# Causal attention of a fused two-layer kernel: head-wise 5 KB writes of the relative scores, a third staging pair, and value products ahead of the turns

## What is computed

```
Q = LN(x) Wq + bq ; K = ctx Wk + bk ; V = ctx Wv + bv        (per head, 512 x 16)
QEr = Q Er^T                      (512 x 512, Er is 512 x 16)
Srel = skew(QEr)                  (row s shifted so that column t holds Q[s] . Er[511 - s + t])
attn = softmax(causal((Q K^T + Srel) / 4)) ; out = attn V ; x = x + out
```

## Time and profile before

| what | us |
|---|---|
| median of 3 runs | 1227.47 |
| lowest, highest | 1227.22, 1229.96 |
| profiled execution, own time | 1220.86 |
| its span in the trace | 1219.0 |
| mean granted TensorE clock | 0.933 |
| causal stage, first `relative` to last scores | 57 to 358 |

### The profile page before, as it was taken

How to read it: one execution, slowest core, us unless ns; L and a number is a source line. 1 busy time by engine, 2 the same in 40 slices (tenths; PEclk the granted TensorE clock), 3 DMA queues, 4 the chain that set the end, 5 groups by cost and what they waited for, 6 DMA issues and landing times. The chain is left out here.

```text
span 1219.0 us, 22097 instructions
## 1 busy us (share of the span) xinstructions
PE 1068.6 (88%) x6978; PEld 665.8 (55%) x6979; DVE 661.2 (54%) x1993; ACT 635.3 (52%) x1245; POOL 199.1 (16%) x466
## 2 busy tenths in 40 slices
PE   7999999999997868999999991547999999987487
PEld 5556555555554567999999991312333333325254
DVE  4428778777776521121111102857666666774697
ACT  2457677776742422222223330516777777762797
POOL 0000000000000022122223210002222223230232
PEclk9959999999898979999999996869999999998798
DMA  5098899888966637566666654253111111100001
GB/s 181 10 302 280 281 311 293 302 272 287 295 226 225 226 118 278 190 216 216 216 216 221 230 192 147 92 184 109 49 46 48 46 45 45 47 26 9 0 32 39
DMA packets 92239, 199.56 MB, mean 164 GB/s; under 512 B 8392, under 2 KB 49608, under 8 KB 86152
## 3 DMA queue, kind: packets, MB, share of 16 engines
q1 hardware_dynamic: 88424, 188.46, 47.3%
q0 software_dynamic: 3744, 10.23, 2.2%
HBM read 134.82 MB, written 63.83 MB: 163 GB/s over the span
## 5 line engine op out<-in xcount | busy, mean ns | idle before, releaser
L775 DVE CUSTOM_DVE_ANT_0 unused<-mpsS,mask_bias 128x512 bf16<-128x512 f32 x256 | 172.1, 691 | 82.3 <-PE mpsS L708 81.9
L1516 ACT ACTIVATE hT<-ph,w 128x128 f32<-128x128 f32 x312 | 89.0, 368 | 205.1 <-PE ph L1490 186.5
L802 ACT ACTIVATE mPT<-mpsB 128x512 f32<-128x512 f32 x256 | 152.5, 597 | 80.8 <-PE mpsB L715 74.6
L1490 PE MATMUL ph<-xT,w 128*128 128x128 f32 x1248 | 151.1, 281 | 6.2 <-DMA w<-in_w1p 6.0
L1490 PEld LDWEIGHTS ph<-xT,w 128*128 128x128 f32 x1248 | 146.8, 197 | 8.6 <-issue 8.4
L1535 DVE TENSOR_TENSOR xn<-py,b 128x256 f32<-128x256 f32 x39 | 16.6, 425 | 244.9 <-PE py L1500 244.9
L1500 PE MATMUL py<-w,hT 128*128 x624 | 141.2, 379 | 0.7 <-DVE xn L1535 0.7
L650 ACT ACTIVATE scores<-scores,nm 128x512 f32<-128x512 f32 (+3 forms) x256 | 125.4, 554 | 10.5 <-DVE nm L621 10.5
L1500 PEld LDWEIGHTS py<-w,hT 128*128 128x128 f32 x624 | 115.6, 190 | 15.2 <-issue 1.1
L643 ACT COPY stage<-psE 128x1024 f32<-128x1024 f32 (+1 forms) x90 | 78.7, 874 | 83.6 <-PE psE L533 67.6
L708 PE MATMUL mpsS<-mqk 96*128 96x512 bf16 x256 | 100.5, 394 | 20.4 <-DMA mqk<-packed 17.3
(11 more groups left out here) (261 smaller groups left out, 1614.5 us busy)
## 6 DMA issues: line engine op xcount, KB each, us to landing
w<-in_w1p SPq DMA_DIRECT2D x39, 1028.0 KB, 5.6
rel<-stage SPq DMA_DIRECT2D x64, 512.0 KB, 7.5
bias<-rel SPq DMA_DIRECT2D x44, 640.0 KB, 6.0
x<-rel SPq DMA_DIRECT2D x20, 640.0 KB, 5.9
mqk<-packed SPq DMA_DIRECT2D x64, 192.0 KB
rel<-stage SPq DMA_DIRECT2D x32, 256.0 KB, 7.1
w<-in_w2p SPq DMA_DIRECT2D x8, 1024.0 KB, 12.5
b<-in_b SPq DMA_DIRECT2D x39, 128.0 KB, 5.7
```

The lines of the kernel that those rows point to most:

```text
L775: nc.vector.tensor_tensor_reduce(out=unused[:, i, :], in0=psS[i % 2][:, :], in1=mask_bias[:, i, :], scale=1.0, scalar=-3.0e38, op0=ALU.add ...
L802: nc.scalar.activation(PT[r][:, j, :], psB[j % 2][:, :], ACT.Exp, scale=1.0 / 4).then_inc(s_exp, 1)
L1490: mm = nc.tensor.matmul(ph[half][:, q * P:(q + 1) * P], w1[i][:, dk * F + f * P:dk * F + (f + 1) * P], xT[i][:, dk, :], start=(dk == 0), s ...
L1516: g = nc.scalar.activation(hT[i][:, f, :], ph[half][:, q * P:(q + 1) * P], ACT.Gelu, bias=w1[i][:, DK * F + f:DK * F + f + 1])
```

## The change

1. DRAM tensors are per head (eight of 128 x 1280) and each head is written by one DMA of 128 rows of 5 KB; a pair is 2 write DMAs in place of 3. The row pitch of the skewed read is 1279 elements in place of 2559.
2. A read of a head waits for that head's write alone.
3. SyncE's step order becomes: both reads of pair n+4, then both writes of pair n+5. The writes wait for all three units' copies.
4. Staging has three pairs of buffers. The third pair's two heads lie apart (one in x, one in the memory of mask_bias, which the early weights wkv and the heads buffer now share), so for every third pair ScalarE copies each unit with two instructions in place of one. ScalarE waits once a pair, at unit 0, for the two writes of three pairs before.
5. On TensorE, in each unit, `weigh` and (in unit 2) `vals.turn` come ahead of `turn_probs`.
6. SyncE waits for the last writes before it loads wkv.

```diff
-    rel = [dram(f"rel_{r}", (P, 2, REL_W), F32) for r in range(RING)]
+    rel = [dram(f"rel_{r}", (P, REL_W), F32) for r in range(ROUND)]
...
+            STAGES = 3
...
-                vals = Values(ctx, "a")
+                vals = Values(ctx, "a", wkv_flat[:, REL_W:REL_W + S])
...
-                s_wr = [[sem(f"s_wr{r}_{u}") for u in range(NU)] for r in range(RING)]
+                s_wr = [sem(f"s_wr{r}") for r in range(ROUND)]
...
+                def stage_of_head(p, h):
+                    if p % STAGES < 2:
+                        return stage[p % STAGES][:, h, :]
+                    return (spare[:, 2 * REL_W:3 * REL_W], wkv_flat[:, 0:REL_W])[h]
...
                     def read(p):
-                        for u in range(NU):
-                            sp.wait_ge(s_wr[p % RING][u], 16 * (p // RING + 1))
-                        sp.sem_inc(s_seen_sp, 1)
                         for h in range(2):
+                            slot = (2 * p + h) % ROUND
+                            sp.wait_ge(s_wr[slot], 16 * (2 * p // ROUND + 1))
+                            sp.sem_inc(s_seen_sp, 1)
                             if p >= len(bias):
                                 sp.wait_ge(s_soft, piece(p - len(bias), NU - 1, h) + 1)
-                            skewed = bass.AP(rel[p % RING].ap().tensor, P - 1 + h * REL_W, [[2 * REL_W - 1, P], [1, REL_W]])
-                            sp.dma_start(bias[p % len(bias)][:, h, :], skewed).then_inc(s_rd[(2 * p + h) % ROUND], 16)
-
-                    def write(p, u):
-                        cols = slice(512 * u, 512 * u + WU[u])
-                        sp.wait_ge(s_eev, NU * p + u + 1)
-                        if p >= RING:
-                            for h in range(2):
-                                m = 2 * (p - RING) + h
-                                sp.wait_ge(s_rd[m % ROUND], 16 * (m // ROUND + 1))
-                        sp.dma_start(rel[p % RING][:, :, cols], stage[p % 2][:, :, cols]).then_inc(s_wr[p % RING][u], 16)
+                            skewed = bass.AP(rel[slot].ap().tensor, P - 1, [[REL_W - 1, P], [1, REL_W]])
+                            sp.dma_start(bias[p % len(bias)][:, h, :], skewed).then_inc(s_rd[slot], 16)
+
+                    def write(p):
+                        sp.wait_ge(s_eev, NU * (p + 1))
+                        for h in range(2):
+                            slot = (2 * p + h) % ROUND
+                            wait(sp, s_rd[slot], 16 * (2 * p // ROUND))
+                            sp.dma_start(rel[slot][:, :], stage_of_head(p, h)).then_inc(s_wr[slot], 16)
 
                     for n in range(-REL, NP - SOFT):
-                        early, back = pair_at(n, REL), pair_at(n, READ)
-                        if early is not None:
-                            write(early, 0)
-                        if back is not None:
-                            read(back)
-                        if early is not None:
-                            write(early, 1)
-                            write(early, 2)
+                        if (p := pair_at(n, READ)) is not None:
+                            read(p)
+                        if (p := pair_at(n, REL)) is not None:
+                            write(p)
+                    for m in range(NBH - ROUND, NBH):
+                        sp.wait_ge(s_wr[m % ROUND], 16 * (m // ROUND + 1))
...
-                            if late is not None:
-                                turn_probs(late, u)
                             if 0 <= g < NBH // GROUP and u < 2:
...
-                        if n % 2 == 0 and 0 <= n // 2 - 2 < NBH // GROUP:
-                            vals.turn(pe, n // 2 - 2, 0)
+                            if u == 2 and n % 2 == 0 and 0 <= n // 2 - 2 < NBH // GROUP:
+                                vals.turn(pe, n // 2 - 2, 0)
+                            if late is not None:
+                                turn_probs(late, u)
...
                             if early is not None:
-                                if early >= 2:
-                                    act.wait_ge(s_wr[(early - 2) % RING][u], 16 * ((early - 2) // RING + 1))
+                                cols, bank = slice(512 * u, 512 * u + WU[u]), relative_bank(early, u)
+                                if early >= STAGES and u == 0:
+                                    for h in range(2):
+                                        m = 2 * (early - STAGES) + h
+                                        act.wait_ge(s_wr[m % ROUND], 16 * (m // ROUND + 1))
                                 act.wait_ge(s_emm, NU * early + u + 1)
-                                nc.scalar.copy(stage[early % 2][:, :, 512 * u:512 * u + WU[u]],
-                                               relative_bank(early, u)[:, :, 0:WU[u]]).then_inc(s_eev, 1)
+                                if early % STAGES < 2:
+                                    nc.scalar.copy(stage[early % STAGES][:, :, cols], bank[:, :, 0:WU[u]]).then_inc(s_eev, 1)
+                                else:
+                                    nc.scalar.copy(stage_of_head(early, 0)[:, cols], bank[:, 0, 0:WU[u]])
+                                    nc.scalar.copy(stage_of_head(early, 1)[:, cols], bank[:, 1, 0:WU[u]]).then_inc(s_eev, 1)
```

More of the change, by code:

```diff
@@ L363, in build, with __init__ @@
         class Values:
-            def __init__(self, ctx, tag):
+            def __init__(self, ctx, tag, heads=None):
                 self.spread = [sb(ctx, f"spread{tag}{i}", [P, GROUP, NI, CG]) for i in range(2)]
                 self.zeros = sb(ctx, f"zeros{tag}", [P, VW])
-                self.heads = sb(ctx, f"heads{tag}", [P, S])
+                self.heads = sb(ctx, f"heads{tag}", [P, S]) if heads is None else heads
                 self.rinv = sb(ctx, f"rinv{tag}", [P, 2, NI, GROUP])
@@ L444, in causal_attention @@
                 bias = [sb(ctx, f"bias{r}", [P, 2, REL_W]) for r in range(2)]
-                bias.append(x[:, :, :].rearrange("p t d -> p (t d)")[:, 0:2 * REL_W].rearrange("p (a w) -> p a w", a=2))
+                spare = x[:, :, :].rearrange("p t d -> p (t d)")
+                bias.append(spare[:, 0:2 * REL_W].rearrange("p (a w) -> p a w", a=2))
                 scores = [sb(ctx, f"scores{r}", [P, 2, REL_W]) for r in range(3)]
@@ L814, in build @@
             dmask = sb(ctx, "dmask", [P, P], BF16)
-            wkv = sb(ctx, "wkv", [P, 2, DK, D])
+            mask_bias = sb(ctx, "mask_bias", [P, NI, S])
+            wkv_flat = mask_bias[:, :, :].rearrange("p i s -> p (i s)")
+            wkv = wkv_flat[:, 0:2 * DK * D].rearrange("p (n k e) -> p n k e", n=2, k=DK)
             s_wkv = sem("s_wkv")
@@ L957, in build @@
                     causal_attention(er, qf, identb, dmask)
-            mask_bias = sb(ctx, "mask_bias", [P, NI, S])
             maskT = sb(ctx, "maskT", [P, NI, S], BF16)
```

## The result

The changed kernel takes 1252.48 us (median of 4 runs, 1250.87 to 1253.32) against 1227.35 for the kernel before (4 runs): 25 us slower, ratio 1.0201 with a 95% interval of 1.018 to 1.0223. Its profiled execution took 1252.84 us, its span is 1251.1. The forecast was 19 us faster.

What follows compares the result with a forecast made beforehand. It took a DMA loop of work and gap at 9.09 us a pair as the bound; DMA 7.7 + 0.3 = 8.0 and engines 8.2 gave 8.3 a pair, 24 intervals 19 us faster, 1208.5 us, range 1197 to 1222.

Steps and rivals of the forecast that it cites:

- What bounded the kernel: DMA loop of writes, landing and next reads: 9.09 us a pair, where the engines can do about 8.2.
- Head-wise writes and reads: In SyncE's DMA loop, head 1's write flows while head 0's read is issued; gap falls from 1.1 us to 0.3 a pair.
- SyncE's order: In SyncE's queue, unit 0's write moves behind the reads; 3.4 us of slack before the bias is used, so cost 0.
- The slower rival: DMA engines idle at each turn because SyncE's write stands behind the reads: 10.0 us a pair, 1249 us; chance 0.08.
- Its deciding point: The slower rival holds where line 505's wait for ACT (ScalarE) passes 4.4 us a pair; it was 0.4.
- the signs named for a wrong forecast: 9 us a pair with DVE (VectorE) waiting for bias or psT, or SyncE waiting over 4 us a pair for ACT (ScalarE).
- 5 KB rows: In the write DMAs, longer rows save between 0 and 0.45 us a pair, 0.2 taken; the skill's packet price gives 0.12.
- The rule against the split: Skill's rule of at least 1 MiB per DMA, against 640 KB here; set aside while the queue is never empty.
- The third staging pair: Removes ACT's (ScalarE's) 15.5 us of waits; split copies add 0.13 us a pair, covered by its waits for PE (TensorE).
- The order on TensorE: Products and finished-head turns ahead of probability turns: between +0.2 and -0.2 us a pair, 0 taken.
- The clock: Granted clock averaged 0.73 from 296 to 315, costing 0 to 5 us; gone in the sum, may come back.
- 54 engine-us a MB for reads: DMA work of reads alone, from share 0.991 of 16 engines over 3 us for 0.88 MB.

Runs made afterwards that it cites:

- experiment 3: Changed kernel with SyncE's queue interleaved head by head (read head 0, write head 0, read head 1, write head 1): 1210.30 us, ratio 0.9884 to the kernel before.
- experiment 5: The interleaved kernel of experiment 3 with TensorE's old order: 1203.85 us, ratio 0.9826 to the kernel before.
- experiment 7: The interleaved kernel of experiment 3 with two staging pairs in place of three, so no split copies: 1211.23 us, ratio 0.9892 to the kernel before.
- experiment 8: The interleaved kernel of experiment 3 with each head's write in three DMAs of 2, 2 and 1 KB rows: 1211.39 us, ratio 0.9897 to the kernel before.
- experiment 10: The interleaved kernel of experiment 3 with two staging pairs and TensorE's old order: 1208.70 us, ratio 0.9852 to the kernel before.
- experiment 6: Changed kernel with both heads' writes waited for ahead of both reads: 1272.01 us, ratio 1.0373 to the kernel before.
- experiment 4: Kernel before with unit 0's write issued behind the reads instead of ahead of them: 1271.86 us, ratio 1.0383 to the kernel before.
- experiment 1: Kernel before with only the new TensorE order: 1225.92 us, ratio 1.0016 to the kernel before.

## Why the prediction was wrong, point by point

**What bounded the kernel** was read rightly: a loop of write, landing and read at 9.09 us a pair over engines that can do about 8.2. Experiments 3 and 5 took VectorE's and ScalarE's waits for DMA away and found 8.35 and 8.18.

**The step that failed** is the pair "Head-wise writes and reads ... so I take 0.3" and "SyncE's order ... cost 0". The DMA loop was made up as work plus gap: 7.7 + 0.3 = 8.0. That holds only if the next pair's data are in the queue while a landing is waited for. The part on SyncE's order compared data with their deadline two steps later and found slack, but never asked what is left in the queue while SyncE waits. The answer was in the earlier trace rows: three writes stand between two reads, and by the code one of them is the next pair's unit 0. With reads first, the only thing behind head 1's write is head 0's read; measured, that is 9.58 us from writes to writes in the turn shown, and 10.0 a pair on average. The gap did not shrink to 0.3 but grew: by their shares, the DMA engines stood idle for 0.11 x 9.09 = 1.0 us a pair before and 0.18 x 10.0 = 1.8 in the changed kernel. Experiment 3 shows that a loop of at most 8.35 was reachable with the same DMAs: there head 1's landing is waited for with a read and a write in the queue. Whether it could go down to 8.0 no run shows, since there the engines set the pace.

**The slower rival** (chance 0.08, 1249 us) named the right mechanism, "before, unit 0's write filled that place", and came within 4 us. That its sum of 7.7 + 1.1 + 1.2 gives the measured 10.0 is luck: the 1.2 was waiting for copies, and in 100 to 340 no write waits for one. Its deciding point was wrong in the same way: it wanted ScalarE's copies to be late by 4.4 us a pair. The writes waited, in order, behind the reads. Here a queue whose head waited for a landing held up data that were ready. With that condition dropped, nothing in the rows spoke against the rival, and it should have carried most of the chance. Of the signs named for a wrong forecast, VectorE's waits for bias (28.3 us) and for psT (11.6) came; the one that was to mark this rival, SyncE waiting for ScalarE, did not.

**5 KB rows:** 0.2 us a pair taken, 0.2 to 0.3 measured (experiments 3, 7, 8 and 10). The estimate by the Trainium skill ("DMA: Bandwidth & Descriptors", Why small descriptors are slow) was 0.12: right in sign, low in size. Between the kernel before and the changed one the work of a MB stayed as it was within what the shares can tell, 0.82 x 16/0.265 = 49.5 engine-us against 0.89 x 16/0.289 = 49.3.

**The rule against the split** (the Trainium skill, "DMA: Bandwidth & Descriptors", Rules for kernel authors, at least 1 MiB per DMA for bandwidth) was weighed and set aside. No run has a DMA of 1 MiB in this chain. What the runs show is that DMAs of 640 KB reached 410 GB/s in the changed kernel (row at the end), and that DMAs of 256 and 128 KB for a head's write cost nothing that shows in the interleaved one (experiment 8). Experiment 6 is about the waits and not about the size of a DMA: with DMAs of 640 KB in both, waiting for both heads' writes before reading costs 20 us more than waiting for each.

**The third staging pair:** the waits of 15.5 us went, as forecast, and the split copies cost nothing that shows (experiment 7 has none, and the time of experiment 3). But the time did not follow: VectorE waited 7.7 us longer for its biases, and experiment 6, with the third pair and without head-wise reading, is as slow as experiment 4, with neither. With the interleaved queue the stages are 1 and 3 us shorter with the pair than without it, within what single traces can tell.

**The order on TensorE:** taken as 0 between -0.2 and +0.2 a pair. It is +0.17, near the upper bound, where DMA does not bind (experiments 3 and 5, and again 7 and 10); behind the slow loop nothing shows in the medians (experiment 1). The reason given, VectorE idle because its copy starts later, is what the waits show: 10.9 us in 28 places in place of 2.1 in one.

**The clock** was put at up to 5 us inside the 9.09 that would be gone with the waits. In the changed kernel the falls were longer, not gone. A stretch at full clock, 2.4 GHz, of the kernel before (21 pairs) and one of the changed kernel (5 pairs):

```profile
106.55:294.50 187.95, 180.84 (x1637) 107.72 (x1636) 144.02 (x439) 135.66 (x241) 7.20 (x10) 1.00 0.88 290
```

```profile
148.05:198.55 50.50, 46.75 (x397) 26.84 (x392) 34.33 (x106) 32.52 (x63) 1.45 (x2) 1.00 0.81 260
```

That is 8.95 us a pair and 10.1 (9.6 in another stretch of three pairs, 230 to 258.75), so the loop is slower without any fall of the clock. The clock adds to it, as a later stretch of the changed kernel shows:

```profile
271.00:272.00 1.00, 0.64 (x12) 0.34 (x6) 0.33 (x1) 0.31 (x1) 0.00 (x0) 1.00 0.96 399
272.00:273.00 1.00, 0.57 (x2) 0.43 (x3) 1.00 (x3) 1.00 (x3) 0.00 (x0) 1.00 0.31 128
...
275.00:276.00 1.00, 1.00 (x5) 1.00 (x6) 0.43 (x4) 0.00 (x0) 0.00 (x0) 0.50 1.29 410
```

TensorE is busy for 0.6 of the time from 271 to 273, where VectorE waits 2.2 us for a bias, and at 275 its clock stands at 0.50, which is 1.2 GHz. Over 240 us a mean clock of 0.94 in place of 0.98 is at most 0.04 x 240 = 10 us more, an estimate from above, since TensorE does not bound every moment; so up to 10 of the 22 us go by way of the clock. In experiment 3, with the order mended, it was 1.00 from 100 to 340. This is in line with falls that come behind waits; no run holds the waits and changes the clock.

## What to carry to other kernels

Where a queue that waits in order both writes data out and reads them back, write down what is still in flight at the moment it waits for a landing: that, and not the sum of the bytes or the slack to the deadline, says whether the transfer engines run dry. Put ready writes of the next piece ahead of, or between, reads that wait. Larger rows and a third staging pair did not save the changed kernel, and finer waits, worth 20 us in it, covered only part of what the order lost. A DMA share of 0.89 did not decide whether DMA was the bound: in the kernel before VectorE and ScalarE waited for DMA at that share, and with the order mended the same share moved 301 GB/s in place of 289 and neither waited for it. Whether a second queue for the writes would serve as well was not tried.

## What the runs showed of the hardware that was not expected

A busy DMA engine can move little. In the changed kernel the half microsecond 218.5 to 219, where the second head's read has just begun, shows a share of 1.03 at 154 GB/s, and 216.5 to 217, in the first head's read, 410 GB/s at 0.99:

```profile
216.50:217.00 0.50, 0.50 (x16) 0.38 (x8) 0.50 (x1) 0.00 (x0) 0.00 (x0) 1.00 0.99 410
```

By the times of the issues, both half microseconds of the turn with a high share and a low rate, 215 to 215.5 (0.88 at 113 GB/s) and 218.5 to 219, lie where a read has just begun. Why was not tried. One reading is that the share counts packets that wait for memory as busy; no run shows it. Either way a share is not a measure of the bytes moved, and the prediction's 54 engine-us a MB for reads, worked out from a share of 0.991, may hold waiting beside work.
